# Another schedule for the last group of each half: earlier decays, weight tiles by sequence, and six of the next half's token turns inside it

## What is computed

```python
proj = einsum('bld,pd->blp', LN(x), in_proj_w)      # gate 4096 | x 4096 | B 1024 | C 1024 | dt 64
xBC  = silu(causal_conv4(proj[x, B, C]))
dt   = softplus(dt + dt_bias);  dA = exp(-exp(A_log) * dt)
state = state * dA + (dt * x) outer B;  y = state @ C      # 64 heads of 64, 8 groups of B and C
y    = rmsnorm_per_group(y + D * x) * norm_weight * silu(gate)
s    = y @ out_proj_w                                # 2048 tokens x 1024
# beside it: small projections of x -> 50 Sinkhorn steps on 4x4 matrices per token,
# a branch product, and the elementwise combination of both with s
```

## Time and profile before

| | us |
|---|---|
| median of 3 runs | 3021.14 |
| lowest, highest | 3020.88, 3022.29 |
| the profiled execution | 3022.99 |
| its span in the trace | 3021.5 |
| PE busy in the span | 2972.3 (98%) |
| DVE, ACT, POOL busy | 2138.0, 1717.2, 834.1 |
| mean granted TensorE clock, share of full | 0.996 |

### The profile page before, as it was taken

One profiled execution on the slowest core, in us unless ns is written; L12 is line 12 of the kernel. 1 busy time (PEld: TensorE's weight loads), 2 busy tenths in 40 slices (PEclk: granted clock), 3 DMA queues, 4 the chain that ended last, 5 costly groups with the idle time before them and its releaser, 6 DMA issues.

```text
span 3021.5 us, 44616 instructions
## 1 busy us (share of the span) xinstructions
PE 2972.3 (98%) x14160; PEld 2320.8 (77%) x14160; DVE 2138.0 (71%) x2678; ACT 1717.2 (57%) x3744; POOL 834.1 (28%) x561
## 2 busy tenths in 40 slices
PE   8999999999999998999999999999999999999998
PEld 7777777777777776777777777777776888888876
DVE  7676667676766676767667676767677878678767
ACT  5666575657566675475665757575665232244443
POOL 3222332333323355323233223323233100001112
PEclk9999999999999999999999999999999999999999
DMA  3425342524334353534342434343353544466655
GB/s 130 156 105 181 106 160 91 181 99 152 139 111 174 122 192 100 162 119 140 112 175 92 158 111 174 101 150 138 129 190 107 178 145 145 146 209 213 223 198 179
DMA packets 126872, 444.99 MB, mean 147 GB/s; under 512 B 21360, under 2 KB 25584, under 8 KB 110352
## 3 DMA queue, kind: packets, MB, share of 16 engines
q1 hardware_dynamic: 118352, 421.17, 40.5%
q0 software_dynamic: 4640, 16.78, 1.5%
q10 hardware_dynamic: 3744, 5.51, 0.6%
HBM read 397.92 MB, written 45.48 MB: 147 GB/s over the span
## 4 chain that ended last, share of the span: by engine, by line
PE 75%; issue 6%; DMA 5%; POOL 4%; DVE 4%; ACT 3%; SPq 1%; ACTq 0%; DVEq 0%; POOLq 0%
PE bank L1125 16%; PE bank L1127 15%; PE bank L1126 15%; PE bank L1170 8%; PE bank L1414 6%; PE bank L1415 6%; PE bank L1416 6%; POOL gate L506 2%; PE bank L1138 2%; DMA acc<-in_w_out 2%; PE bank L1156 1%; DMA y_scratch<-gate 1%; DMA units<-cum_scratch 1%; POOL nrstd L494 1%; DVE acc L862 1%
## 5 line engine op out<-in xcount | busy, mean ns | idle before, releaser
L1125 PE MATMUL bank<-x_hi,w_hi 128*128 128x512 f32 x2576 | 1017.3, 395 | 8.4 <-DVE acc L862 4.8
L1127 PE MATMUL bank<-x_hi,w_lo 128*128 128x512 f32 x2576 | 1001.3, 389 | 0.0
L1126 PE MATMUL bank<-x_lo,w_hi 128*128 128x512 f32 x2576 | 1001.0, 389 | 0.0
L1125 PEld LDWEIGHTS bank<-x_hi,w_hi 128*128 128x128 f32 x2576 | 484.4, 188 | 122.4 <-issue 19.5
L1127 PEld LDWEIGHTS bank<-x_hi,w_lo 128*128 128x128 f32 x2576 | 484.3, 188 | 101.9
L1126 PEld LDWEIGHTS bank<-x_lo,w_hi 128*128 128x128 f32 x2576 | 484.8, 188 | 95.2
L862 DVE SCALAR_TENSOR_TENSOR acc<-bank,conv_w,acc 128x511 f32<-128x511 f32 (+2 forms) x576 | 429.8, 747 | 179.6 <-ACT acc L635 150.5
L844 DVE TENSOR_TENSOR w_lo<-w_raw,w_hi 128x1024 fp32r<-128x1024 f32 x160 | 227.8, 1424 | 357.9 <-ACT w_hi L619 357.7
L488 POOL TENSOR_TENSOR sums<-sums,sq 128x512 f32<-128x512 f32 x96 | 191.1, 1991 | 911.4 <-ACT sq L695 911.4
L903 DVE TENSOR_TENSOR units<-units,bc 128x2560 f32<-128x2560 f32 x128 | 387.1, 3025 | 54.3 <-ACT units L682 54.3
L672 ACT ACTIVATE units<-units,falls 128x128 f32<-128x128 f32 x1024 | 325.9, 393 | 149.7 <-DMA units<-cum_scratch 149.7
(11 more groups left out here) (169 smaller groups left out, 3253.3 us busy)
## 6 DMA issues: line engine op xcount, KB each, us to landing
units<-cum_scratch SPq DMA_DIRECT2D x128, 1280.0 KB, 8.2
w_raw<-in_w_in SPq DMA_DIRECT2D x160, 512.0 KB, 3.7
xbc<-y_scratch SPq DMA_DIRECT2D x126, 512.0 KB, 3.6
acc<-in_w_out SPq DMA_DIRECT2D x126, 256.0 KB, 3.8
y_scratch<-gate SPq DMA_DIRECT2D x30, 1024.0 KB, 5.3
xbc<-in_x SPq DMA_DIRECT2D x16, 512.0 KB, 5.5
units<-in_x SPq DMA_DIRECT2D x16, 512.0 KB, 3.7
rstd_b<-rc_scratch SPq DMA_DIRECT2D x16, 512.0 KB, 4.2
```

Source lines behind the costliest of these rows:

```text
L1125: pe.matmul(out, w_hi[m % 2][:, k, :], hi, start=(k == 0), stop=False)
L1126: pe.matmul(out, w_hi[m % 2][:, k, :], lo, start=False, stop=False)
L1127: mm = pe.matmul(out, w_lo[m % 2][:, k, :], hi, start=False, stop=(k == KT - 1))
```

## The change

1. **Table `LAST`.** The decays are loaded from slot 1 (before 4), `exps` stand at slots 3 to 17 (before 6 to 18), `weigh` at 8, 9, 10, 11, 14, 15, 17, 18 (before 8, 10, 12, 13, 15, 16, 18, 19), `turn_x` and `mult` of units 0 to 5 a slot or two earlier; units 6 and 7 are still multiplied at 20. A new list `finish` puts `finish_y` of units 2 and 3 at slot 14. The table serves both halves.
2. **Weight tiles by sequence** (`tile_of`), in group 7 alone: slots 16 to 19 are tile 8 and tile 9 on sequence 0, then tile 8 and tile 9 on sequence 1 (before: tile 8, 8, 9, 9). Sequence 0 of `x_hi` and `x_lo` is then free after slot 17, weight tile 9 is wanted at slot 17 (before 18), and the split of the next group's tile 0 stands in slot 18 behind `gate_in`.
3. **Six turns in group 7** (before two): turns 0 and 1 ahead of slot 18's product, 2 in its middle, 3 ahead of slot 19's, 4 and 5 in its middle; `high` and `low` of them in slots 17 and 18 of ACT's and DVE's lists. The front begins at turn 6. The small products stand behind turns 9 and 11 there, the channel sums behind turn 13, and the drained steps of the other engines start with tile 3.
4. **Token tiles and small weights earlier on SP.** Tiles 0 to 6 are loaded in group 7 (before 0 to 4), the small weights at slot 14 into `acc` (before in the front, into a decay buffer).
5. **Order on SP in every first group:** the slot's weight load ahead of `load_bx`; the two stores of group 7's `y` at slot 1 (before ahead of slot 0).

```diff
-LAST = Plan(cb=[4, 7], load=[4, 5, 6, 7, 12, 12, 15, 15],
-            exp=[6, 7, 8, 9, 10, 11, 12, 12, 14, 14, 15, 15, 17, 17, 18, 18],
-            attn=[8, 10, 12, 13, 15, 16, 18, 19], turn=[7, 7, 11, 11, 14, 14, 17, 17],
-            mult=[11, 11, 14, 14, 17, 17, 20, 20], gate_from=CONV_SLOTS)
+LAST = Plan(cb=[4, 7], load=[1, 1, 5, 5, 11, 11, 13, 13],
+            exp=[3, 4, 5, 6, 7, 8, 9, 10, 12, 12, 13, 14, 15, 16, 17, 17],
+            attn=[8, 9, 10, 11, 14, 15, 17, 18], turn=[7, 7, 10, 10, 12, 12, 16, 16],
+            mult=[10, 10, 12, 12, 16, 16, 20, 20], finish=[10, 10, 14, 14, 16, 16, 20, 20], gate_from=CONV_SLOTS)
+SMALL_FILL = [[5, 9], [9, 11]]
+SUMS_TURN = 13
-AHEAD_LOAD = [8, 8, 12, 15, 19]
-AHEAD_STATS = [10, 11, 14, 17]
-AHEAD_SCALE = [11, 12, 15, 18]
+AHEAD_LOAD = [8, 8, 11, 15, 17, 18, 19]
+AHEAD_STATS = [10, 11, 13, 17, 19]
+AHEAD_SCALE = [11, 12, 14, 18]
+SMALL_LOAD = 14
+AHEAD_TURNS = 6
...
+    def tile_of(s, half, plan):
+        m, q = divmod(s, SEQS)
+        if turns_ahead(half, plan) and m >= TILES - SEQS:
+            q, m = m - (TILES - SEQS), TILES - SEQS + q
+        return m, q
...
             for s in range(SLOTS):
-                if plan is FIRST and s < NT:
-                    load_bx(half, s)
                 if s % 2 == 0:
                     ahead = s // 2 + 2
                     if ahead < TILES:
                         load_w(g, at, ahead)
                     elif not ends_all(half, plan):
                         load_w(g + 1, after(at, plan), ahead - TILES)
+                if plan is FIRST and s < NT:
+                    load_bx(half, s)
+                if plan is FIRST and half and s == 1:
+                    drain(piece, half - 1, LAST.store[0])
...
+                if turns_ahead(half, plan) and s == SLOTS - 3:
+                    high(half + 1, 0)
+                    high(half + 1, 1)
+                if turns_ahead(half, plan) and s == SLOTS - 2:
+                    split_hi(g + 1, 0, used=1)
+                    high(half + 1, 3)
                 for group in open_groups(g, s, half, plan, before):
                     piece(*group)
+                if turns_ahead(half, plan) and s == SLOTS - 3:
+                    high(half + 1, 2)
+                if turns_ahead(half, plan) and s == SLOTS - 2:
+                    high(half + 1, 4)
+                    high(half + 1, 5)
...
-            for n in range(2 * half, 2 * NT):
-                t, h = divmod(n, 2)
-                if half and n == 2:
+            for n in range(AHEAD_TURNS * half, 2 * NT):
+                if half and n == AHEAD_TURNS:
                     drain(piece, half - 1, SLOTS, SLOTS + 1)
-                    pe.wait_ge(dtx_done, UNITS * g)
                 turn_stream(half, n)
-                if half and h:
-                    drain(piece, half - 1, SLOTS + t, SLOTS + t + 1)
-                if n in (5, 9):
-                    small_products(n // 4 - 1)
+                if half and n == SUMS_TURN:
+                    drain(piece, half - 1, SLOTS + 1)
+                if n in SMALL_FILL[half]:
+                    small_products(SMALL_FILL[half].index(n))
```

More of the change, by code:

```diff
@@ L134, with __init__ @@
 class Plan:
-    def __init__(self, cb, load, exp, attn, turn, mult, gate_from):
+    def __init__(self, cb, load, exp, attn, turn, mult, gate_from, finish=None):
         self.cb, self.bc = cb, [s + 1 for s in cb]
         self.load, self.exp, self.attn, self.turn, self.mult = load, exp, attn, turn, mult
-        self.square = [s + 1 + u % SEQS for u, s in enumerate(mult)]
-        self.gate = [max(s + 1, gate_from + 1 + u) for u, s in enumerate(mult)]
+        self.finish = finish if finish is not None else mult
+        self.square = [s + 1 + u % SEQS for u, s in enumerate(self.finish)]
+        self.gate = [max(s + 1, gate_from + 1 + u) for u, s in enumerate(self.finish)]
         self.norm = max(mult) + 3
@@ L477, in gate_y @@
             pool.wait_ge(y_done, UNITS * g + u + 1)
-            pool.wait_ge(gate_done, GATE_SLOTS * g + u + 1)
+            pool.wait_ge(gate_done, GATE_SLOTS * g + (u + 2 if ahead and u == 5 else u + 1))
             pool.tensor_tensor(part, part, y[:, u % 2, :], ALU.mult).then_inc(gated, 1)
@@ L602, in step @@
                     piece(*group)
-                if plan is LAST and half + 1 < HALVES:
+                if turns_ahead(half, plan):
                     for t in due(AHEAD_STATS, s):
@@ L716, in high @@
             if half:
-                act.wait_ge(proj_done, SLOTS * half * GROUPS - (1 if t < NT // 2 else 0))
+                act.wait_ge(proj_done, SLOTS * half * GROUPS - (2 if t < NT // 2 else 0))
             act.wait_ge(e.turned, n + 1)
@@ L769, in step @@
                     tanh(g, s - 1)
-                split_next_hi(g, s, ends_all(half, plan))
+                if not (turns_ahead(half, plan) and s == SLOTS - 2):
+                    split_next_hi(g, s, ends_all(half, plan))
                 if s < CONV_SLOTS:
@@ L776, in step @@
                 else:
-                    gate_in(g, at, s)
+                    gate_in(g, at, s, half, plan)
                     if ends_all(half, plan) and s == SLOTS - 2:
@@ L782, in step @@
                         tap_params(after(at, plan))
+                if turns_ahead(half, plan) and s == SLOTS - 3:
[4 more added lines that the diff above has]
+                    high(half + 1, 3)
                 for group in open_groups(g, s, half, plan, before):
                     piece(*group)
+                if turns_ahead(half, plan) and s == SLOTS - 3:
[3 more added lines that the diff above has]
+                    high(half + 1, 5)
         def front(half):
             e = early_of[half]
-            for t in range(NT):
-                if t == 0 and half:
+            for t in range(AHEAD_TILES if half else 0, NT):
+                for i in SCALE_AT[half].get(t, []):
+                    normalise(half, i)
+                if half and t == AHEAD_TILES:
                     act.wait_ge(proj_done, SLOTS * half * GROUPS)
@@ L793, in front @@
                     act.activation(small_hi, small_raw, ACT.Copy).then_inc(e.small_step, 1)
-                for i in SCALE_AT[half].get(t, []):
-                    normalise(half, i)
                 high(half, 2 * t)
@@ L1075, in step @@
                     silu(g, s - 1)
-                split_next_lo(g, s, ends_all(half, plan))
+                if not (turns_ahead(half, plan) and s == SLOTS - 2):
+                    split_next_lo(g, s, ends_all(half, plan))
                 for group in open_groups(g, s, half, plan, before):
@@ L1298, in step @@
             for s in range(SLOTS):
-                if plan is LAST and half + 1 < HALVES and s == SLOTS - 1:
+                if turns_ahead(half, plan) and s >= SLOTS - SEQS:
                     pe.wait_ge(bc_done, SEQS * (g + 1))
-                    for n in range(2):
+                    pe.wait_ge(dtx_done, UNITS * (g + 1))
+                    turns = ((0, 1), (2,)) if s == SLOTS - SEQS else ((3,), (4, 5))
+                    for n in turns[0]:
                         turn_stream(half + 1, n)
-                if plan is not FIRST:
-                    project(g, s)
+                    project(g, s, (0, KT // 2), half=half, plan=plan)
+                    for n in turns[1]:
+                        turn_stream(half + 1, n)
+                    project(g, s, (KT // 2, KT), half=half, plan=plan)
+                elif plan is not FIRST:
+                    project(g, s, half=half, plan=plan)
                 elif s > 1:
```

79 lines of the change are left out of this document (49 added, 30 removed).

## The result

| | us |
|---|---|
| before: median of 9 runs (lowest, highest) | 3021.14 (3016.27, 3023.0) |
| after: median of 9 runs (lowest, highest) | 3011.04 (3007.93, 3014.91) |
| ratio after to before, 95% interval | 0.9962 (0.9954 to 0.997) |
| profiled execution before, its span | 3022.99, 3021.5 |
| profiled execution after, its span | 3007.93, 3006.3 |

The changed kernel is 10.1 us faster by the medians. One run of the kernel before in the first experiments took 5262.6 us at a mean granted clock of 0.672; the ratios leave it out. The two profiled executions differ by 15.1 us: the one of after is the lowest of its nine runs. So the places where the gain arises are read as the *shift* of one and the same product of PE from trace to trace, and only the medians say how much is left at the end.

A forecast was written before the change was run, and what follows sets the result against it. PE, busy 98% of the span, was taken as the bound, with time lost to waits and lower clock. Terms 6.1 + 4.35 + 0 + 0 = 10.5 us took the median from 3021.14 to 3010.6, range 3003.5 to 3017.0.

The forecast's parts named there:

- End of group 15: Last products of group 15: the wait for the weighing and the lower clock go, 6.1 us gained, bounds 4.45 to 6.15.
- Group 7 and the front: Unit 7's product through the second front: 4.35 us gained, small product 0 near 1158 and still slow, bounds 0.5 to 6.6.
- 5.8 of now: PE's idle time before small product 0 in the kernel before, set against about 7 us expected after the change.
- Slot 4: Half 1's first group: SP's order gains, POOL's scaling beside early costs; 0 net, bounds -1.0 to +4.8 us.
- The contention: Before slot 4: POOL's scaling slows two or three DVE operations of early, 0.9 to 1.1 us each, 1.8 to 3.3 in all.
- the clock's 2.4 us: Half slot behind slot 4: 5.25 us where full clock needs about 2.8; 2.5 us of clock to gain with the wait.
- the price of the old SP order: Before slot 4: ACT waits 2.40 us for weight tile 2; a new order would give 2.3 us, and 2.5 of clock.
- Inside groups 7 and 15: Slots within both groups: nothing gained or lost, with little cover; 0, bounds -4 to 0 us.
- Rivals 2 and 3: 2: new wait in group 7, about 3015, chance 0.22; 3: ACT late in slots 12 to 16, 3024.6, chance 0.07.
- Rival 1: Before slot 4: the scaling misses the chain or costs nothing, 4.8 us more, 3005.8 or 3003.5; chance 0.17.
- Rival 4: End of group 15: the table changes nothing PE sees, 4 to 5 us gain left, 3017; chance 0.04.

The follow-up runs named there:

- the first experiments: The series that measured table_end, table_both, sp_order and the changed kernel run again; the kernel before had a median of 3021.84 us beside it.
- table_end: Kernel before with the new table for group 15 alone, all else old: 3017.58 us, ratio 0.9983.
- old_sp_order: Changed kernel with SP's old order back, bx loads ahead of the weight tiles and both stores of y early: 3023.31 us, ratio 0.9996.
- bx_ahead: Changed kernel with load_bx ahead of the weights again, stores of y still at slot 1: 3009.75 us, ratio 0.9966.
- short_scaling: Changed kernel with six of the eight POOL scalings of group 7's gate left out: 3010.95 us, ratio 0.9957.
- hold_scaling: Changed kernel with POOL's scaling of group 7's gate held until DVE's subtraction ahead of the softmax is done: 3016.05 us, ratio 0.9979.
- late_alone: Changed kernel with the scaling behind the first group's eight mixings and the stores in SP's slot 9: 3007.69 us, ratio 0.9946.
- table_both: Kernel before with the new table in both halves and nothing else of the change: 3014.65 us, ratio 0.9974.
- tile4_ahead: Changed kernel with tile 4's statistics a slot or two earlier and its normalisation in slot 18 on DVE: 3008.2 us, ratio 0.9946.
- the two last edits: Tile 4 normalised ahead on DVE, and the scaling moved behind the mixings, both on the changed kernel: 3000.91 us, then 3002.96 when measured again.
- the second: The changed kernel unaltered, run again beside the kernel before: 3009.93 us against 3021.84, ratio 0.9953.
- late_scaling: tile4_ahead with the scaling behind the first group's eight mixings and the stores in SP's slot 9: 3000.91 us, ratio 0.994.
- late_again: late_scaling measured once more, unaltered: 3002.96 us, ratio 0.9931.
- sp_order: Kernel before with SP's new order alone, weight tiles ahead of bx loads and stores of y later: 3017.83 us, ratio 0.9985.

## Why the prediction came out

The medians moved from 3021.14 to 3011.04 where 3010.6 was forecast. Point by point:

- **End of group 15**, 6.1 predicted: 5.85, 5.86 and 5.85 us in the changed kernel, `table_end` and the changed kernel run again. Both halves of the term, the 4.45 us wait and the clock behind it, went as said. The difference is a new wait of 0.45 us for the output product's split, which stands behind the weighing as named.
- **Group 7 and the front**, 4.35 predicted: 4.48. Tile 4 is normalised at 1154.40 (1155.5 predicted), small product 0 starts at 1158.41 (1158) and stays slow, PE idles 5.7 us ahead of it (6 to 8 predicted). The "5.8 of now" that the prediction sets this against is misread: it holds the 1.27 us before the channel sums, which lie behind small product 0; the old waits between unit 7's product and small product 0 are 4.56 us. How close the size came is partly luck: in six more traces of the same front (the changed kernel again, `old_sp_order`, `bx_ahead`, `short_scaling`, `hold_scaling`, `late_alone`) it gives 3.9 to 5.5 us, mostly because small product 0 takes 4.1 to 5.3 us. That the front's chain and not the product sets this was shown from both sides: the table alone gains nothing at slot 4, tile 4 ahead gains 5.2 at `small_to_tokens`.
- **Slot 4**, 0 predicted: 0.07 at its start, in one pair of traces. Slot 4 stands 15.42 to 16.04 us behind `small_to_tokens` with the old order on SP and the old schedule (before, `table_end`, `table_both`), and 15.35 to 15.82 in the changed kernel, run again, `bx_ahead` and `tile4_ahead`. The scaling ran from 1185.36 to 1197.02, ending 1 us later than said, and the wait is 2.69 us, within what was said. The contention was bounded at 1.8 to 3.3 us and measures 2.2 to 2.6. The steps that pay were only in part the ones named: of the two tensor_tensor steps of `early` on SBUF alone the subtraction was slowed and the 128x192 sum was not, and the weight split, which the prediction left out, paid 0.83 us. Two more things were mis-sized. The prediction took the clock's 2.4 us with the wait, as all or nothing; in fact it is open at such a wait (next section): 2.44 us came back in the profiled run, 1.26 in the run again, 0.84 in `bx_ahead`. And the price of the old SP order was read off the old trace, where the scaling was over in time. With the sums moved behind turn 13 it is 11.75 us and not 5.4. The zero is what part 5 saves, 11.75 us with the clock, against a loss of about the same size, most of which the same change had made by ending the scaling later. Here the sum was right because both parts were in it, not because the parts had their sizes.
- **Inside groups 7 and 15**, 0 predicted: no wait of PE of over 1.3 us there, and PE's shift stays at +0.26 from slot 0 to slot 8 of group 7 and at -8.32 from slot 0 to 8 of group 15. The silu of slot 11 came at 1098.64 (1098 predicted). Rivals 2 and 3 didn't occur.
- **Rival 1** (3003.5 to 3005.8 if the scaling doesn't meet the chain) is what the two last edits build; its price of 4.8 us is 2.6 for the wait and up to 2.4 of clock. Rival 4 falls with `table_end`.

The terms that the traces show add to 5.85 + 4.5 + 0.1 and 0.8 to 2.4 of clock, 11.2 to 12.8 us, and the front's own spread widens that. The medians gave 10.1 in the first comparison and 11.9 in the second, the ratios 11.5 (interval 9 to 14) and 14.2; between these the runs can't decide. The mechanism and the two large terms came out as said; that the median met the forecast within 0.5 us is luck.

## What to carry to other kernels

When a step is moved later, follow what waits for its result through the queues it is issued on: the scaling that ended 6 us later was harmless for itself and would have cost 11.75 us (without part 5) through a store that stood ahead of a weight load. Elementwise work of POOL that nobody waits for belongs where DVE's short steps are not on the path. Here the collision was not avoided by shifting the work some 5 us against the chain (`hold_scaling`), but by moving it to a stretch in which POOL is idle for long enough. Where one run's noise is as large as an edit's gain, read the shift of one product across the place in the two traces, and take a second trace of the same kernel: stretches with a lower clock differed by up to 1.9 us between traces of the same work.

## What the runs showed of the hardware

**A lower clock is not certain behind a wait.** PE in `late_scaling` and in `late_again`, the same program, with nearly the same waits in the second front (2.42 and 1.88 us; 2.27 and 1.81). `late_again` reaches the front 3 us later, so its windows are shifted by 3 us (PE's busy time and instructions, granted clock, DMA share and GB/s). First `late_scaling`, then `late_again`:

```profile
1147.00:1153.00 6.00, 2.77 (x24) 1.00 0.49 175
1153.00:1159.00 6.00, 4.93 (x38) 1.00 0.27 87
```

```profile
1150.00:1156.00 6.00, 2.94 (x26) 0.91 0.51 175
1156.00:1162.00 6.00, 4.99 (x24) 0.52 0.30 87
```

One run stays at 2.4 GHz, the other falls to 1.2 GHz and does 24 products where the first does 38, and its tile 4 edit is worth 1.9 us less. Behind slot 4's wait of 2.7 us it is the same: granted 1.00 between 1202 and 1208 in the changed kernel, 0.72 in the changed kernel run again (wait 2.71), 0.77 in `bx_ahead` (2.70), and 1.00 in the 6 us behind the wait of 2.70 in `tile4_ahead`. With a wait of 0.8 to 1.03 us there (`sp_order`, `short_scaling`, `late_scaling`, `late_alone`, `late_again`) no profiled run fell, with 3.3 or more (before, `table_end`, `table_both`, `old_sp_order`, `hold_scaling`) all did. A term for the clock near such a wait is a range, not a number.

**What DVE pays beside POOL's scaling does not grow with the size of the step.** Beside the scaling a copy of 128x128 took 1.20 us for 0.23, one of 128x32 1.14 for 0.18, one of 128x8 1.03 for 0.16, a split of 128x1024 2.27 for 1.23, a weighing of 128x2560 3.92 for 2.82: 0.9 to 1.1 us each, over three hundredfold in size. Others paid less, or a different price each time: a product of 128x64 0.78 for 0.22 in `hold_scaling`, the split 1.76 where the scaling had just begun (after), a silu of 128x512 from 0.82 (after) to 1.61 (`late_scaling`) for 0.68. Reductions (0.21 and 0.21) and the steps that read a PSUM bank (the convolution, 2.31 and 2.31) paid nothing. The Trainium skill ("GPSIMD Engine Reference", Specifications) says that the two share SBUF interfaces, in contention with 2-port modes or two SBUF inputs. The traces agree on most steps and not on all: the sum of 128x192 has two SBUF inputs and took 0.36 us beside the scaling in all five traces that have it there, and 0.36 without. No run here shows why it was spared. The price is the traces'.
